# Attention block on one core: logits of two steps in one go, and the out-projection in two parts

## The reference

```
xn = layernorm(x, g_in);  q = (xn @ Wq) * scale;  k, v = split(xn @ Wkv), with a null row ahead
sim = q @ k.T + bias;  masked by causal and by mask;  attn = softmax(sim)
out = (attn @ v).reshape(b, n, 1024) @ Wo;  return x + layernorm(out, g_out)
```

## Time and profile before

| what | value |
|---|---|
| median of three runs | 1200.64 us |
| the profiled execution itself | 1201.94 us |
| its span in the trace | 1200.1 us |
| PE busy | 1087.0 us (91%) |
| POOL busy | 805.3 us (67%) |
| DVE busy | 736.3 us (61%) |
| ACT busy | 673.8 us (56%) |
| mean granted TensorE clock | 0.965 |

### The profile page before, as it was taken

How to read it: one execution, slowest core, us unless ns; L and a number is a source line. 1 busy time by engine, 2 the same in 40 slices (tenths; PEclk the granted TensorE clock), 3 DMA queues, 4 the chain that set the end, 5 groups by cost and what they waited for, 6 DMA issues and landing times.

```text
span 1200.1 us, 43028 instructions
## 1 busy us (share of the span) xinstructions
PE 1087.0 (91%) x14464; PEld 949.5 (79%) x14464; DVE 736.3 (61%) x3536; ACT 673.8 (56%) x2666; POOL 805.3 (67%) x1488
## 2 busy tenths in 40 slices
PE   4799999999999999999999999999999999999975
PEld 4787888888888887888888888888888888888864
DVE  4666666665666656756665765656666656666551
ACT  3656555655555656655655655655655646655551
POOL 3667766666776767766666766767767767767672
PEclk9899999998999999999999999999999999999997
DMA  8111121122121121121022122012112112111100
GB/s 226 51 47 62 43 64 55 37 64 62 41 64 56 37 64 62 41 65 62 30 64 64 39 63 65 28 64 65 52 50 64 37 56 64 56 47 46 46 28 26
DMA packets 51548, 67.72 MB, mean 56 GB/s; under 512 B 13888, under 2 KB 25664, under 8 KB 51392
## 3 DMA queue, kind: packets, MB, share of 16 engines
q1 hardware_dynamic: 49280, 63.21, 17.0%
q10 hardware_dynamic: 2112, 2.10, 0.6%
HBM read 40.11 MB, written 16.78 MB: 47 GB/s over the span
## 4 chain that ended last, share of the span: by engine, by line
PE 67%; DVE 11%; issue 9%; ACT 5%; POOL 3%; DVEq 1%; POOLq 0%; ACTq 0%
PE ps_pv L424 31%; PE ps_proj L430 22%; PE ps_pv L411 10%; PE ps_s L387 3%; DVE wt L508 3%; DVE xt_lo L562 3%; ACT exp_bot L663 2%; DVE y_stats L521 2%; ACT exp_top L663 1%; POOL small L804 1%; DVE logit_bot L492 1%; ACT xt_hi L693 1%; PE ps_proj L448 1%; DVE x_stats L533 1%; DVE logit_top L492 1%
## 5 line engine op out<-in xcount | busy, mean ns | idle before, releaser
L430 PE MATMUL ps_proj<-xt_hi,wq_hi 128*128 128x256 f32 x1024 | 299.7, 293 | 0.1
L771 POOL TENSOR_TENSOR bias_b<-bias_c,mask_add 128x256 f32<-128x256 f32 (+1 forms) x512 | 296.9, 601 | 0.1
L430 PE MATMUL ps_proj<-xt_hi,wq_lo 128*128 128x256 f32 x1024 | 289.6, 283 | 0.0
L430 PE MATMUL ps_proj<-xt_lo,wq_hi 128*128 128x256 f32 x1024 | 289.2, 282 | 0.0
L663 ACT ACTIVATE exp_bot<-logit_bot,neg_max 128x129 f32<-128x129 f32 x512 | 201.5, 400 | 60.0 <-DVE neg_max L492 57.5
L780 POOL TENSOR_TENSOR w_nrm<-exp_bot,w_inv 128x256 f32<-128x256 f32 x256 | 156.6, 612 | 112.4 <-DVE w_inv L501 109.9
L424 PE MATMUL ps_pv<-wo_hi,o_hi 128*128 128x512 f32 x512 | 211.9, 414 | 4.7 <-DVE o_lo L513 4.7
L424 PE MATMUL ps_pv<-wo_lo,o_hi 128*128 128x512 f32 x512 | 206.0, 402 | 0.0
L676 ACT ACTIVATE y_nrm<-ps_pv,small 128x512 f32<-128x512 f32 x64 | 49.9, 779 | 276.7 <-POOL small L807 276.7
L424 PE MATMUL ps_pv<-wo_hi,o_lo 128*128 128x512 f32 x512 | 204.6, 400 | 0.0
L430 PEld LDWEIGHTS ps_proj<-xt_hi,wq_hi 128*128 128x128 f32 x1024 | 194.1, 190 | 10.0 <-issue 5.3
(11 more groups left out here) (61 smaller groups left out, 2042.4 us busy)
## 6 DMA issues: line engine op xcount, KB each, us to landing
x_in<-in_x_dram SPq DMA_DIRECT2D x32, 512.0 KB, 4.4
x_res<-in_x_dram SPq DMA_DIRECT2D x64, 256.0 KB, 2.8
out_dram<-y_out SPq DMA_DIRECT2D x64, 256.0 KB, 2.1
v_rep<-v_raw SPq DMA_DIRECT2D x256, 32.0 KB, 1.9
w_raw<-in_L_cond_Wq_dram ACTq DMA_DIRECT2D x4, 512.0 KB, 8.0
w_raw<-in_L_cond_Wo_dram SPq DMA_DIRECT2D x4, 512.0 KB, 7.3
mask_u<-in_mask_BxS_bk_dram SPq DMA_DIRECT2D x32, 32.0 KB, 4.1
bias_c<-in_fside_16xSxS_dram SPq DMA_DIRECT2D x4, 128.0 KB, 7.7
```

What stands on the lines that cost most here:

```text
L430: mm = pe.matmul(ps[:, 0:TOK], w[:, k, cols], xt[:, k], start=(j == 0), stop=(j == len(todo) - 1))
L771: ins = nc.gpsimd.tensor_tensor(out_, bias, key_mask, ALU.add)
```

## The change

The out-projection is cut: its first 18 matmuls stay at step 7 of the batch, and the last 6 go to step 8, on PE behind the scores of that visit and ahead of its FRONT parts. DVE is regrouped by visits: at the even step the logits of both steps of the visit, with the copy of the visit's first FRONT part between them where no heads are due; then the statistics of the out-projection, heads_lo, the other copies, the transposes of both steps of the visit before, and the inverse of the even step; at the odd step the copies of its FRONT parts and the inverse of the odd step. POOL does at the odd step: normalize the even one, two masked biases for the next visit, normalize the odd one. ACT and SP are not edited.

```diff
-PLAN = {"pv": 6, "heads": 6, "out": 7, "stats": 8, "norm": 8, "add": 10}
+PLAN = {"pv": 6, "heads": 6, "out": 7, "out_rest": 8, "stats": 8, "norm": 8, "add": 10}
 # PE
-            def project_out(batch):
+            def project_out(batch, some):
-                for j, (o, w, i) in enumerate(todo):
+                for j, (o, w, i) in list(enumerate(todo))[some]:
-                mm.then_inc(o_done, 1)
+                if some.stop is None:
+                    mm.then_inc(o_done, 1)
                         values(p, batch, back)
+                    if t % 2 == 0:
+                        for batch, back in due("out_rest", p, t, first, last):
+                            project_out(batch, slice(18, None))
                     for f, slot, kind, i in front_parts(p, t, first, last):
                         front(f, slot, kind, i)
...
-                        project_out(batch)
+                        project_out(batch, slice(0, 18))
+                        if last and back == 3:
+                            project_out(batch, slice(18, None))
 # DVE
+                    parts = list(front_parts(p, t, first, last))
+                    if t % 2 == 0:
+                        early = parts[:1] if not list(due("heads", p, t, first, last)) else []
+                        if t < CP:
+                            logits(n, t)
+                            for part in early:
+                                front(*part)
+                            logits(n + 1, t + 1)
+                        for done in due("stats", p, t, first, last):
+                            out_stats(*done)
+                            out_mean_var(*done)
+                        for batch, back in due("heads", p, t, first, last):
+                            for g in range(4):
+                                heads_lo(batch, g)
+                        for part in parts[len(early):]:
+                            front(*part)
+                        for lag in (LAG_T, LAG_T - 1):
+                            if live(t, LAG_T, first, last):
+                                transposed(n - lag, 2 * GB * p + (t - LAG_T) // CB, (t - lag) % CP)
+                    else:
+                        for part in parts:
+                            front(*part)
...
+                        inverse(n, t)
 # POOL
-                    if t < CP and not (last and t == CP - 1):
-                        masked_bias(n + 1, 2 * p + (t + 1) // CG, (t + 1) % CP)
-                    if live(t, LAG_NORM, first, last):
-                        normalize(n - LAG_NORM, t - LAG_NORM)
+                    if t % 2 and t < CP:
+                        normalize(n - 1, t - 1)
+                        if not (last and t == CP - 1):
+                            for ahead in range(1, 3):
+                                masked_bias(n + ahead, 2 * p + (t + ahead) // CG, (t + ahead) % CP)
+                        normalize(n, t)
```

More of the change, by code:

```diff
@@ L38 @@
 WBLOCKS = (BOT + TOP) // BLK
-PLAN = {"pv": 6, "heads": 6, "out": 7, "stats": 8, "norm": 8, "add": 10}
-PLAN_63 = PLAN | {"add": 8}
+PLAN = {"pv": 6, "heads": 6, "out": 7, "out_rest": 8, "stats": 8, "norm": 8, "add": 10}
+PLAN_63 = PLAN | {"out_rest": 7, "add": 8}
 TAIL = 5
-LAG_SUM, LAG_NORM, LAG_T = 1, 1, 2
+LAG_T = 2
 FRONT = {
@@ L842, in _ @@
             masked_bias(0, 0, 0)
+            masked_bias(1, 0, 1)
             x_rstd_of(1)
```

## The result

The changed kernel takes 1379.75 us (median of 4 runs, 1377.64 to 1383.28) against 1200.76 us before: a ratio of 1.150, 95% interval 1.144 to 1.156. It is slower, as forecast; 1336 us was predicted, within 1240 to 1400. The profiled execution took 1378.65 us, with a span of 1376.9 us and a mean granted clock of 0.918.

The account below looks back on a forecast made before the run. PE, busy 91% of the span, bounds the kernel. Two chains add 3.96 us a group, +119 us over some 30 groups on 1201.9, giving 1321; the clock adds 15: 1336 us, range 1240 to 1400.

Parts of the forecast that it names:

- The removed wait: PE's waits for wt ahead of the values matmuls: every one can go, at most 61.6 us.
- x1: First half: PE stands 2.9 us ahead of these matmuls for the copy of q7, 85 to 95 us in all.
- Out-projection, first half: PE stands another 0.8 us ahead of the 18 matmuls, which end at 20.17 us, against 18.07 before.
- Second half: Steps t = 4 to 7: PE stands 2.4 us ahead of the 18 matmuls, which end at 18.96, against 17.10.
- predicted group of 39.13 us: Both halves of a group as one chain from the scores: 20.17 and 18.96 us, +3.96 against before.
- lower bound of 0.03 us: Hand-over between engines, read from the copy's end to x1; upper bound 0.28, 0.05 to 0.1 mostly used.
- 15 hand-overs: Handing over between engines in a group: at the skill's upper figure about 0.4 us more, 12 us longer in sum.
- The clock: PE clock drops: 0.71 us a group as now, plus 0.5 taken at the stretch ahead of kv, +15 us.
- Nothing takes its place: Rival: the wait for wt goes and q7's copy is ready when x0 ends; 1140, or 1119 without drops; chance 0.09.
- Both stretches lose the clock each time: Rival: a clock drop in each half of each group, +72 us on 1321, 1393; no separate chance given.
- One half only: Rival: first half as computed, second chain hidden by room on DVE and POOL; +53, 1255 us; chance 0.12.
- the 6 late matmuls are worth nothing: Scores start 1.45 us earlier, worth nothing at t = 0 and 4 if DVE waits for q5 anyway.

Follow-up runs that it names:

- e5: The changed kernel with 12 extra matmuls, results never read, in each of PE's two standings of a group (not in the first pair): 1340.03 us.
- e1: The changed kernel with the copy of the visit's first part (q5 or q0) moved from between the logits to behind the statistics: 1209.47 us.
- e3: The changed kernel with out_norm on ACT behind the exponentials of the even step instead of ahead of them: 1226.04 us.
- e9: The changed kernel with no copy between the logits, out_norm behind the even step's exponentials, and both biases ahead of the normalizations: 1150.98 us.
- e2: The changed kernel with the out-projection whole again at step 7, DVE and POOL still regrouped: 1378.60 us.
- e4: The kernel before with only the out-projection cut 18 and 6, the 6 behind the scores; DVE and POOL as before: 1209.22 us.
- e10: e9 with the out-projection whole again at step 7: 1175.66 us.
- e11: e9 with the copy of the visit's first part between the two logits again: 1190.55 us.
- e6: The changed kernel with the inverse of the even step behind the query copies of the odd step instead of ahead of them: 1357.56 us.

## Why the prediction was right, and by how much it was off

The mechanism, both places and their order were right. **The removed wait:** gone wholly, as said (no row for wt is left). **x1:** 2.9 us predicted, 3.08 seen, 92.3 us in all against 85 to 95. The copy of q7 was to end 10.21 us after the scores and ended at 10.22. **Out-projection, first half:** 0.8 us of standing predicted; kv's last matmul runs into the out-projection with no wait in the group shown, because values at the lower clock took 2.86 us where 1.56 was put in and filled the gap. The 18 matmuls began at 16.38 instead of 15.81. **Second half:** 2.4 us predicted, 2.82 seen. The logits of 7 began 13.37 us after the scores (668.07 to 681.44), 0.35 behind what the sum had for them, and waited 0.20 us of that for a bias; heads_lo began at 14.08.

**What was mis-sized.** The predicted group of 39.13 us, at the full clock, is about 40.2: 20.50 for the first half and, in the mean, 19.7 for the second (both from e5; the changed kernel's own halves without a drop take 20.49 and 19.69). So the chains were taken 1.1 us a group too short, 32 us in all. In a second half without the unexplained idle time, 19.53 us, the sum of the two halves is 0.9 too short, and where the group shown can be followed, the hand-overs make most of it: the rows with 0.2 to 0.3 us were the typical ones, not the one at x1. In the group shown the trace was still 0.12 us ahead of the sum when the inverse of step 1 ended (13.45 us after the scores against 13.57); then came 0.21 us to the logits of step 2, logits at 0.8 in place of 0.68 each, and 0.22 to heads_lo, and two heads were done at 16.28 in place of 15.76. The lower bound of 0.03 us was itself misread: in the trace of before the copy of q7 ends at 609.73 and x1 starts at 609.79, 0.06 later.

The Trainium skill (Advanced Engine Details and Errata, Miscellaneous Facts) gives 50 to 100 ns for reading a semaphore; by its upper figure, 15 hand-overs would add an estimated 0.4 us a group. The trace agrees in direction and shows about twice as much, 0.9 us.

The clock: 0.71 + 0.5 = 1.21 us predicted a group, 41.46 - 40.2 = 1.3 measured. That the size came out is in part luck, for the place did not. The forecast put all of it in the first half. There the drop came in 28 of 30 groups and was mostly hidden (0.3 us), but for the 7 groups with a longer one, and the mean is 0.7 us. The other 0.6 us come from the second half: a drop there, put among the rivals, came in 11 of 30 groups and cost 20.69 - 19.53 = 1.16 us in the group shown, for the late matmuls have no cover.

Of the 43 us between forecast and profile, then, 32 are the chains and 1 or 2 the clock. Some 9 lie outside the 30 groups, which I had taken as unchanged: from the scores of the last group to the end it is 67.1 us (1309.8 to 1376.9), against 59.1 before (1141.0 to 1200.1).

**The rivals.** "Nothing takes its place" (1140, or 1119 without drops) did not happen here. It was to hold if the copy of q7 came early; e1 and e3 show that this is not enough by itself (1209 and 1226), and e9, with the biases early too, took 1151. "Both stretches lose the clock each time" (1393) came nearer the measured time than the forecast did, but by too much clock on too short a chain: it charged 2.39 us a group more than before, where 0.6 was measured. "One half only" (1255) did not happen; both decided. That the 6 late matmuls are worth nothing holds in the changed kernel (e2) and in the one before (e4), and not in e9 (e10).

## What to carry to other kernels

When two steps are taken together, write out for each engine what now stands *behind* the first thing that waits; a 0.4 us copy ahead of a statistics cost 170 us, since three engines did their urgent work behind it, and still 40 us where out_norm was out of the way (e11). Urgent small things (statistics, scales) go ahead of whatever can wait, and large things that only have to be done some time (out_norm) go behind what the bottleneck is fed with. The row that names who ended a wait names the last link; move that link alone and most of the wait moves on (e6), cut the chain nearer its start and it is nearly gone (e1, e3).

## What the runs showed of the hardware

Matmuls that nobody needs, put where PE would stand, made the kernel 40 us faster (e5): the mean granted clock rose from 0.918 to 0.980. The small values matmuls are slowed by the lower clock as well, 2.86 us in place of 1.64. A drop came behind both long standings of the group shown, and none in the half before it (19.53 us), which stands 2.86 us ahead of its out-projection as well. Over 30 groups of the changed kernel it was 28 first and 11 second halves; in the kernel before, 14 first halves of 30, which took 19.4 us in place of 18.07, one of them 20.9. Why one of two alike stretches is followed by a drop and the other not, no run here shows.
